# Adapter's output product cut into two 64-partition tiles of 128 tokens, whose PSUM banks are exchanged behind a semaphore

## The reference, cut to what matters

```python
base_out = jnp.einsum('bti,oi->bto', x, W) + b        # 512 x 512
A  = lora_As[adapter_mapping]                         # per sequence, 512 x 16
Bm = lora_Bs[adapter_mapping]                         # per sequence, 16 x 512
lora_h   = jnp.einsum('bti,bir->btr', x, A)
lora_out = jnp.einsum('btr,bro->bto', lora_h, Bm)     # the adapter's output product
y = base_out + lora_out * SCALING                     # then q, k, v = y @ Wq, Wk, Wv ...
```

## Time and profile before

| what | us |
|---|---|
| median of 3 runs | 171.23 |
| lowest and highest run | 169.52, 172.09 |
| profiled execution, its own time | 172.04 |
| span of the profiled execution | 170.4 |
| PE busy | 146.8 (86%) |
| PE weight loads busy (they overlap) | 126.9 (74%) |
| DVE, ACT, POOL busy | 96.2, 78.8, 76.7 |

### The profile page before, as it was taken

The page is one execution under the profiler, slowest core; times in us unless marked ns, Lnnn a source line. Parts: engine busy times, 40 slices in busy tenths (PEclk is TensorE's granted clock), DMA queues, the critical chain, the costliest instruction groups (busy, mean ns, idle before and its releaser), DMA issues.

```text
span 170.4 us, 4660 instructions
## 1 busy us (share of the span) xinstructions
PE 146.8 (86%) x1792; PEld 126.9 (74%) x1792; DVE 96.2 (56%) x215; ACT 78.8 (46%) x158; POOL 76.7 (45%) x78
## 2 busy tenths in 40 slices
PE   0049899999898998999999998999999899888942
PEld 0048749988887996888899996888997778666620
DVE  0045265170559853545829872676964388756583
ACT  2235072794246987133347961215498341833110
POOL 0360054039694999226221684447209845720000
PEclk9999999999999999999999999999999999999985
DMA  5998867632122201224302361002432100623114
GB/s 169 287 294 241 349 251 258 229 65 59 46 81 61 65 2 44 58 64 133 100 0 81 119 199 61 0 0 89 144 119 102 65 0 2 188 100 129 37 62 185
DMA packets 15143, 19.32 MB, mean 113 GB/s; under 512 B 5714, under 2 KB 10066, under 8 KB 14866
## 3 DMA queue, kind: packets, MB, share of 16 engines
q1 hardware_dynamic: 14146, 16.94, 30.5%
q10 hardware_dynamic: 720, 1.84, 3.3%
q0 software_dynamic: 256, 0.26, 0.6%
HBM read 12.47 MB, written 2.10 MB: 86 GB/s over the span
## 4 chain that ended last, share of the span: by engine, by line
PE 49%; POOL 17%; ACT 12%; DVE 9%; DMA 6%; issue 4%; SPq 1%; POOLq 1%; DVEq 0%
PE bank L928 34%; PE bank L954 7%; DMA xF<-xt 6%; ACT qx L302 5%; POOL ex L514 5%; PE bank L983 4%; PE bank L936 4%; POOL qr L545 3%; POOL Kbd L551 2%; POOL qkc L526 2%; POOL kr L539 2%; ACT kx L302 2%; POOL sm L519 1%; POOL qks L533 1%; DVE cTl L676 1%
## 5 line engine op out<-in xcount | busy, mean ns | idle before, releaser
L519 POOL TENSOR_TENSOR sm<-sm,mx 128x512 f32<-128x512 f32 x16 | 17.1, 1073 | 25.1 <-DVE mx L699 24.9
L954 PE MATMUL bank<-xTh,WTh 128*128 128x256 f32 x64 | 16.9, 304 | 10.9 <-ACT xTh L302 10.9
L514 POOL TENSOR_TENSOR ex<-ex,ri 128x512 f32<-128x512 f32 x16 | 17.7, 1106 | 13.1 <-DVE ri L705 13.1
L302 ACT COPY qx<-bank 32x512 f32<-32x512 f32 x32 | 18.5, 577 | 5.7 <-PE bank L928 5.3
L954 PEld LDWEIGHTS bank<-xTh,WTh 128*128 128x128 f32 x64 | 11.8, 205 | 11.3 <-issue 11.0
L694 DVE TENSOR_TENSOR sm<-bank,mixed 128x512 f32<-128x512 f32 x16 | 10.6, 675 | 16.6 <-PE bank L928 16.6
L368 ACT ACTIVATE ex<-sm 128x512 f32<-128x512 f32 x16 | 10.2, 635 | 18.7 <-POOL sm L519 18.5
L928 PE MATMUL bank<-yTh,Wqh 128*128 128x256 f32 x64 | 18.3, 285 | 0.0
L928 PE MATMUL bank<-yTh,Wql 128*128 128x256 f32 x64 | 17.9, 280 | 0.0
L928 PE MATMUL bank<-yTl,Wqh 128*128 128x256 f32 x64 | 17.9, 280 | 0.0
L954 PE MATMUL bank<-xTl,WTh 128*128 128x256 f32 x64 | 16.6, 293 | 0.4 <-DVE xTl L643 0.4
(11 more groups left out here) (97 smaller groups left out, 364.1 us busy)
## 6 DMA issues: line engine op xcount, KB each, us to landing
RS<-RL SPq DMA_DIRECT2D x32, 136.0 KB, 2.0
xF<-xt SPq DMA_DIRECT2D x8, 256.0 KB, 6.2
xres<-xn SPq DMA_DIRECT2D x8, 256.0 KB, 3.2
out<-x SPq DMA_DIRECT2D x8, 256.0 KB, 2.1
Wqn<-wq ACTq DMA_DIRECT2D x2, 512.0 KB, 9.4
Wn<-w SPq DMA_DIRECT2D x1, 1024.0 KB, 4.9
Wqn<-wo SPq DMA_DIRECT2D x1, 1024.0 KB, 4.8
x<-small SPq DMA_DIRECT2D x1, 904.0 KB, 6.9
```

The costliest lines, as they stand in the source:

```text
L302: return nc.scalar.copy(dst, src)
L514: nc.gpsimd.tensor_tensor(ex[:, j], ex[:, j], ri[:, j, :, None].broadcast_to((P, 2 * NG, T)), ALU.mult).then_inc(normed, 1)
L519: nc.gpsimd.tensor_tensor(sm[:, j % 2], sm[:, j % 2], mx[:, j, :, None].broadcast_to((P, 2 * NG, T)), ALU.subtract).then_inc(shifted, 1)
L954: nc.tensor.matmul(FR[c // 2][:, (c % 2) * TOK:(c % 2 + 1) * TOK], WT[u][:, k, P * c:P * (c + 1)], xT[r][:, k], start=first, stop=False, s ...
```

## The change

`y_adapter(g, 0)` and `y_adapter(g, 1)` keep their places in PE's list but get other contents. A full product over 128 partitions and 256 tokens becomes two products, one for each half e: partitions 64 e to 64 e + 63 with tokens 128 e to 128 e + 127. The blocks left out are those in which `hT` is zero. Per call of `y_adapter` there are now 4 products of 64 x 128 by 128 tokens (it was 2 of 128 x 128 by 256 tokens).

With h = 0, half e = 0 writes bank 0 and half e = 1 writes bank 1; with h = 1 the two halves exchange their banks. Before h = 1, PE waits for a new semaphore `y_half`, which the last product of h = 0 raises. Both increments of `y_ps` come from the last two products of h = 1, first for bank 0, then for bank 1. Before, the first one came at the end of h = 0.

```diff
             def y_adapter(g, h):
-                pe.wait_ge(h_sb, g + 1)
-                for c in (2 * h, 2 * h + 1):
-                    dst = FR[h][:, (c % 2) * TOK:(c % 2 + 1) * TOK]
-                    i = nc.tensor.matmul(dst, B1[g % 2][:, P * c:P * (c + 1)], hT[:], start=False, stop=True, skip_group_check=True)
-                i.then_inc(y_ps, 1)
+                if h:
+                    pe.wait_ge(y_half, g + 1)
+                else:
+                    pe.wait_ge(h_sb, g + 1)
+                for n in range(2):
+                    for e in ((1, 0) if h else (0, 1)):
+                        rows, b = slice(P // 2 * e, P // 2 * (e + 1)), e ^ h
+                        i = nc.tensor.matmul(FR[b][:, n * TOK + P * e:n * TOK + P * (e + 1)],
+                                             B1[g % 2][rows, P * (2 * b + n):P * (2 * b + n + 1)], hT[rows, P * e:P * (e + 1)],
+                                             start=False, stop=True, skip_group_check=True)
+                        if h and n:
+                            i.then_inc(y_ps, 1)
+                if h == 0:
+                    i.then_inc(y_half, 1)
```

More of the change, by code:

```diff
@@ L149, in program @@
             sem, "WT_h WT_l Wq_h Wq_l Wkv_h Wkv_l Wo_h Wo_l BT_l xT_h xT_l yT_h yT_l cT_l".split())
-        h_ps, h_sb, y_ps, q_ps, q_sb, kv_ps, kv_sb, kx_sb, k_sin, q_sin, k_cos, q_cos = map(
-            sem, "h_ps h_sb y_ps q_ps q_sb kv_ps kv_sb kx_sb k_sin q_sin k_cos q_cos".split())
+        h_ps, h_sb, y_half, y_ps, q_ps, q_sb, kv_ps, kv_sb, kx_sb, k_sin, q_sin, k_cos, q_cos = map(
+            sem, "h_ps h_sb y_half y_ps q_ps q_sb kv_ps kv_sb kx_sb k_sin q_sin k_cos q_cos".split())
         k_rope, q_rope, kbd_sb, vs_ps, vbd_sb = map(sem, "k_rope q_rope kbd_sb vs_ps vbd_sb".split())
```

## The result

| | before | after |
|---|---|---|
| median of 4 runs, us | 170.53 | 174.48 |
| lowest and highest | 169.52, 172.09 | 173.68, 175.15 |
| profiled execution: its own time, span | 172.04, 170.4 | 175.15, 173.5 |

The ratio is 1.025, with a 95% interval from 1.0163 to 1.0337: slower by 2.5%, where 0.6% was forecast, and outside the range (170.3 to 174.0). Whether it is more than 2% the interval leaves open. The two profiled executions differ by 3.1 us in their spans. These I can lay out stretch by stretch; the rest, up to the medians' 3.95, comes further down.

A forecast was written before the change was run, and what follows sets the result against it. PE was taken as nearly half the chain, the rest alternating among POOL, ACT, DVE and DMA. Group terms +0.06, +0.47, -0.50 and +0.97 summed to +1.00 us on 171.23, forecasting 172.2, range 170.3 to 174.0.

The forecast's parts named there:

- Tiles side by side: The new product's records on PE: the two alternating tiles run at once, 0.0524 us per record, as in scores.
- the wait: PE waiting between the product's halves for its own first half: 0.38 us, bounds 0.22 and 0.49.
- the entry: PE's switch into the 64-partition form ahead of the product: 0.09 us.
- Group 1, +0.47: Adapter product, group 1: the first signal takes 1.53 us against 1.06, so ACT, DVE and kv come 0.47 us later.
- Group 2, -0.50: Adapter product, group 2: PE's own time counts, its stretch falling from 2.91 to 2.41 us, a gain of 0.50.
- Group 3, +0.97: Adapter product, group 3: the signal comes after the transposes, so ACT starts at 117.90 instead of 116.93, 0.97 us later.
- Group 0, +0.06: Adapter product, group 0: ACT and DVE come 0.27 us later, 0.2 covered by slack, leaving 0.06 us.
- A: Rival: PE counts everywhere, so its savings of 1.25 us remain, giving 170.0 us; chance 0.10.
- B: Rival: the product's tiles run in turn at 0.11 us per record, +3.9 us, giving 175.1; chance 0.08.
- C: Rival: PE's form switches and wait cost their dear ends, wait 0.49, +1.7 us, giving 172.9; chance 0.12.
- D: Rival: group 3's 0.97 us is made up behind it by slack in a later stage, giving 171.3; chance 0.10.
- E: Rival: PE loads the second half's weights early, exchange 0.22 us, +0.62, giving 171.9; chance 0.60 shared with the forecast.

The follow-up runs named there:

- POOL held back: Changed kernel, new form in all groups, with POOL's Wkvl made to wait until all four Wql of DVE are done: median 171.67 us, ratio 1.0083.
- quarters: Old kernel with the new form in group 0 alone and POOL's Wkvl split into four quarter-size instructions: median 171.51 us, ratio 1.0045.

## Why the prediction was wrong

By its own steps:

- **Tiles side by side, 0.0524 us per record; the wait 0.38; the entry 0.09.** These were right: 0.78 between the halves' starts (0.80), records of 0.272, and the stretches ahead of groups 1 and 3 longer by 0.08 and 0.10.
- **Group 1, +0.47.** Measured 0.39 + 0.08 = +0.47. That it fits to the hundredth is luck. The 1.53 us had no hand-over to ACT in it, while the 1.06 beside it had, so ACT came 0.47 + 0.08 = 0.55 later. DVE's four pieces then took 1.66 us instead of 1.74, since the third ACT piece no longer waits for bank 1; "without a break" was wrong there. The stretch from kv(1) to product(2) gives nothing of it back, as the chain over POOL in the rows had it.
- **Group 2, -0.50.** Measured -0.60 + 0.04 = -0.56.
- **Group 3, +0.97.** Measured 0.82 + 0.10 = +0.92, and moving the transposes took off the 0.44 that they should.
- **Group 0, +0.06.** This is the step that failed, the overlap of DVE with POOL: measured +1.77, and 2.09 with group 0 alone. The working was that ACT and DVE come 0.27 us later, "of which 0.2 is covered by the slack". ACT came 0.36 later after the product, and that would indeed have been covered: with POOL held back, q(0) was early. But I let DVE's list shift rigidly and POOL's stand still. Between the two `y_low` calls stand two Wql, and at their side was POOL's Wkvl of 2.7 us, and only 0.7 us lay between the last Wql's start (24.27) and Wkvl's (24.97). From product(0), the last Wql came 0.36 us later (4.22 for 3.86) and Wkvl 0.87 sooner (3.69 for 4.56): 0.56 of this since the second Wql, itself later, no longer stretched Wkvh, and 0.31 since the load of Wkv had landed sooner in this execution. The warning was in the trace: the last Wql was 1.16 us long where its equals were 0.69, and Wkvh 1.60. I hadn't asked what made these two longer, and I had no row of POOL in group 0.

Of the rivals, A (PE counts everywhere) fell with groups 1 and 3. B's time, 175.1, is near the measured one, but its mechanism isn't there: a record takes 0.05 us and not 0.11. C, D and E fell too: the wait cost 0.39 and not 0.49 or 0.22, and behind q(3) nothing is made up. That the time came out near B is chance; the reason is one that none of them had.

On the medians: of the 3.95 us, about 2.8 go with the collision (174.48 to 171.67 with POOL held back). What is left is near the price of the new form by itself, 1.0 us with the same wait in both forms, which is also the prediction's sum without the step that failed (0.94). That too is partly luck: between product(0) and q(3) the profiles of that pair differ by only 0.6 us (100.81 and 100.22), since group 0 gains 0.24.

In the profiled pair the collision's own stretch is only 1.77, since the old form's execution had paid Wkvh's hold of half a microsecond and the clock stayed up in both. The four profiles with the new form in group 0 and a whole, unheld Wkvl have 7.64 to 8.16 us there, the three of the new form with the wait 5.84 to 6.01: 2.0 us apart in the mean. So 0.8 of the 2.8 us isn't in this stretch. The lower clock, 1.5 us in one of these four profiles, could give part of it; how often it falls they are too few to say, and that stays open.

## What to carry to other kernels

Before moving one engine's work by a few tenths of a microsecond, look at what runs beside it on the other: here a DVE instruction with two SBUF inputs, caught by a POOL one, ended 0.55 us after that one's end, however long it was. A record that is longer than its equals (1.16 for 0.69) marks such a meeting before it gets dear; a semaphore took the long hold away, and shorter POOL instructions made it short. When a product is split to make PE faster, ask when its first result is signalled: groups 1 and 3 paid for the later signal directly and group 0 through the collision, and only group 2, where PE was the link, gained.

## What the runs showed that I had not expected

- The hold: 2.48 to 2.85 us for a subtraction of 0.69, ended by the end of POOL's instruction, and 1.21 with quarters.
- How small a shift goes with it: in the kernel before, with POOL's Wkvh 2.88 us after the product the longest Wql took 1.16 us and q(0) came at 6.07; with 2.83 it took 2.84, and q(0) came at 8.11. These are two executions.
- An idle time of 1.84 us on PE was followed, in that execution, by 3.4 us at the lower clock, 1.5 us lost; after 2.13 us in another it was the same, and idle times of 1.93 and 2.23 us in two more had no such fall behind them.
